# Member matrices of a graph attention layer: from compares on VectorE to bf16 products on TensorE

## Chip, cores and metric

The kernel runs on one core of a Trainium2 chip. The metric is device microseconds of one execution, the lower the better; the median of several runs is compared.

## What is computed

There are 50,000 nodes x 128 features and 50,000 edges, sorted by target node. The reference, cut to what matters:

```python
h = jnp.maximum(_layernorm(x), 0.0)
q = (h @ Wq + bq).reshape(n, H, C); k = ...; v = ...        # H = 4 heads of C = 32
alpha = jnp.einsum('ehc,ehc->eh', q[dst], k[src]) / math.sqrt(C)
ea = jnp.exp(alpha - segment_max(alpha, dst)[dst])
alpha = ea / (segment_sum(ea, dst)[dst] + 1e-16)
x = x + segment_sum(v[src] * alpha[:, :, None], dst) + (h @ Wskip + bskip)
h = jnp.maximum(_layernorm(x), 0.0)
x = x + second_layer(h)    # W, gathered rows, edge features, sums by target node
```

"Layer 1" of the change's name is the attention layer (the first layer below). The second layer isn't touched.

## The kernel before

**Stages.** The *table stage* loads rows of x in 40 batches (`b`), takes layernorm statistics, projects k and v and stores them to DRAM (`kv_rows`); SP's queue carries its loads and stores (L509, L518) in an order written by hand (`for b in range(PB)`), and DVE and POOL make the index tables beside it (`index_work`, `table_stat_math`). The *first layer* then goes through 500 tiles of 100 target nodes; the edges of a tile lie in one window of 128 edges. Ten tiles make a batch, so there are 50 batches. The *second layer* follows.

**The member matrix.** For each tile, `member` [128 edges, 100 nodes] has a 1 where the edge's target is the node. DVE builds it by an is_equal of the edge's relative node (`drel_all`) against an iota: `members`, L1187, for four and for six tiles. PE turns it (`turn_member`, L1891, f32 transposes of groups of 4, 4 and 2 tiles), ACT copies the result from PSUM to `memberT` (`copy_member`, L1666). memberT gathers each edge's q row by a product (`gather_q`, L1903), and member sums the weighted v rows by node (`aggregate`, L1936).

**The order.** Every engine has a function `step0(k)` that lists what it does in step k, and this list is its order: nothing moves past an instruction that waits. One step has work of three batches: k+1 (front: q and members), k (scores) and k-1 (softmax, sums). Each batch's road is: ACT's relu of the normalised rows (L1644), PE's `turn_h` (L1865), ACT's `copy_h` (L1651), PE's `project_q` (bias L1878, product L1882), ACT's `copy_q` (L1658), members and turned members, `gather_q`; DVE's `scores` (L1199) and `head_sums` (L1207) against rows that POOL gathers by indirect DMA (L809, ten per batch); PE's `turn_alpha` (L1910); DVE's eight soft steps (L1222, 1225, 1229, then L1231 to L1241), with ACT's exp (L1672) between the third, numbered 2, and the fourth, numbered 3; PE's `turn_weights` (L1914); DVE's `weigh` (L1247); PE's `skip` (L1923, L1928) and `aggregate` per group; DVE's `finish` (L1259). In every second step DVE also has 14 small steps of layernorm statistics between these.

**Semaphores and banks.** PE raises `A.item` ("front_ready") once for each front product and ACT raises `A.evac` ("front_copied") once for each copy; the numbers within a batch are in `ITEM`. Front products use PSUM banks 0, 1 and 2; a product waits until ACT has copied what stood in the bank:

```python
wait(pe, A.evac, N_ITEM * (k - 1) + ITEM[("m1", "m2")[i]])    # turn_h: banks 0 and 1
wait(pe, A.evac, N_ITEM * (k - 1) + ITEM["q2"])               # project_q, first group: bank 2
```

## Time and profile before

| | |
|---|---|
| median of three runs | 1654.79 us (1652.82, 1654.79, 1658.01) |
| the profiled execution, its span | 1654.16 us, 1652.2 us |
| busy over the span | PE 1468.2 us (89%), DVE 1348.9 (82%), POOL 1082.5 (66%), ACT 1017.2 (62%) |
| granted TensorE clock, mean | 0.979 of full speed |
| first gather of the first layer, and of the second | 301.86 us, 1007.87 us |

Busy shares are means over stages that differ; the rows further below are from single stages. In a timeline a row holds the start, the duration, engine, line, operation, output and input, the count of instructions put together in it, and in brackets the idle time of the engine ahead of it and what ended it. "f32" and "bf16" are the types of the operands; PE's ends are modelled, so neighbouring rows overlap.

### The profile page before, as it was taken

What the parts mean: (1) busy time and instruction counts of PE and PEld (TensorE: products, weight loads), DVE (VectorE), ACT (ScalarE), POOL (GpSimd) and SP (SyncE); (2) the same over time, 40 slices, a digit from 0 to 9 for tenths busy, and PEclk for the clock granted to TensorE, in tenths of its full rate; (3) what the DMA queues carried; (4) which work ended last, traced back from release to release, by engine and by line L of the source; (5) the groups of instructions that cost most, each with busy time, mean ns of one, the idle gap of its engine ahead of it and who ended that gap; (6) DMA issues with size and microseconds to landing.
All of it is one profiled execution on the core that took longest, in us unless ns stands there. A gap on an engine that the chain in (4) does not pass through costs nothing. (4 is left out here: it accounts for less than half of the span.)

```text
span 1652.2 us, 34442 instructions
## 1 busy us (share of the span) xinstructions
PE 1468.2 (89%) x10545; PEld 1262.1 (76%) x10546; DVE 1348.9 (82%) x3688; ACT 1017.2 (62%) x2501; POOL 1082.5 (66%) x1202
## 2 busy tenths in 40 slices
PE   5888888699999999999999984899999999999898
PEld 4667767588888888888888873777777777777776
DVE  8879665299999999999999995677777777777676
ACT  5778888555565655555555622556666666656564
POOL 2554442577777777777777704777777777777774
PEclk9999999899999999999999996999999999999999
DMA  8898888556666666666666616576767666676673
GB/s 217 275 276 309 288 296 268 160 150 184 186 182 186 179 190 174 189 170 187 174 181 181 174 44 164 129 173 163 171 161 162 166 161 159 165 165 159 152 171 94
DMA packets 162552, 302.85 MB, mean 183 GB/s; under 512 B 104113, under 2 KB 107703, under 8 KB 157524
## 3 DMA queue, kind: packets, MB, share of 16 engines
q1 hardware_dynamic: 121503, 201.19, 42.2%
q0 software_dynamic: 40896, 99.90, 24.5%
q8 instruction: 62, 1.02, 0.3%
q14 instruction: 91, 0.75, 0.1%
HBM read 196.84 MB, written 104.12 MB: 182 GB/s over the span
## 5 line engine op out<-in xcount | busy, mean ns | idle before, releaser
L809 POOL DMA_INDIRECT sb_kv<-kv_rows,sb_src_all x500 | 492.9, 986 | 187.4 <-issue 130.7
L837 POOL DMA_INDIRECT sb_kv<-x_rows,sb_src_all x500 | 473.2, 946 | 205.7 <-issue 109.7
L1716 ACT ACTIVATE sb_hn<-sb_xn 100x128 f32<-100x128 f32 x500 | 240.6, 481 | 261.2 <-DMA sb_kv<-x_rows,sb_src_all 198.0
L1719 ACT ACTIVATE sb_vw<-sb_kv 128x128 f32<-128x128 f32 x500 | 239.5, 479 | 0.0
L1644 ACT ACTIVATE sb_hn<-sb_xn,sb_nstat 100x128 f32<-100x128 f32 x500 | 231.5, 495 | 0.0
L1406 DVE COPY sb_hT<-ps_b 128x400 f32<-128x400 f32 x250 | 142.5, 570 | 95.1 <-PE ps_b L2011 93.1
L1803 PE MATMUL ps_b<-sb_w,sb_memberT 128*125 128x256 f32 x800 | 201.2, 390 | 20.0 <-DVE sb_xn L927 12.0
L1666 ACT COPY sb_memberT<-ps_b 100x512 f32<-100x512 f32 x150 | 75.8, 506 | 205.9 <-PE ps_b L1891 205.9
L1803 PEld LDWEIGHTS ps_b<-sb_w,sb_memberT 128*125 128x125 f32 x800 | 146.0, 193 | 43.2 <-issue 16.8
L2011 PE MATMUL ps_b<-sb_member,sb_vw 128*128 128x100 f32 x1000 | 173.5, 278 | 0.0
L2011 PEld LDWEIGHTS ps_b<-sb_member,sb_vw 128*128 128x128 f32 x1000 | 157.0, 198 | 9.8 <-issue 9.8
L2010 PE MATMUL ps_b<-sb_ident,sb_hn 100*128 100x100 f32 x500 | 129.3, 259 | 34.2 <-ACT sb_vw L1719 33.9
L1396 DVE TENSOR_SCALAR sb_member<-sb_iota,sb_drel_all,sb_wdeg_all 128x100 f32<-128x100 f32 x500 | 145.8, 344 | 0.0
L1903 PE MATMUL ps_b<-sb_q,sb_memberT 100*128 100x128 f32 x1000 | 129.4, 276 | 9.5 <-DVE sb_prod L1199 7.6
L1882 PE MATMUL ps_b<-sb_w,sb_hT 128*100 128x128 f32 x1000 | 136.3, 276 | 0.0
L1928 PE MATMUL ps_b<-sb_w,sb_hT 128*100 128x128 f32 x1000 | 136.2, 276 | 0.0
L1882 PEld LDWEIGHTS ps_b<-sb_w,sb_hT 128*100 128x100 f32 x1000 | 126.5, 170 | 5.3
L1928 PEld LDWEIGHTS ps_b<-sb_w,sb_hT 128*100 128x100 f32 x1000 | 126.2, 170 | 5.1
L1903 PEld LDWEIGHTS ps_b<-sb_q,sb_memberT 100*128 100x128 f32 x1000 | 120.1, 192 | 10.4 <-issue 8.2
L1936 PE MATMUL ps_b<-sb_vw,sb_member 128*100 128x128 f32 x1000 | 125.5, 273 | 0.0
L1422 DVE COPY sb_q<-ps_b 128x400 f32<-128x400 f32 x150 | 75.3, 502 | 60.7 <-PE ps_b L2024 60.7
L1602 ACT ACTIVATE sb_q<-sb_kv,sb_pstat 125x128 f32<-125x128 f32 x280 | 119.0, 488 | 7.2 <-DVE sb_pstat L877 7.2
(184 smaller groups left out, 3101.5 us busy)
## 6 DMA issues: line engine op xcount, KB each, us to landing
kv_rows<-sb_kv SPq DMA_DIRECT2D x26, 1120.0 KB
sb_xn<-x_rows SPq DMA_DIRECT2D x50, 507.8 KB
sb_xn<-in_x SPq DMA_DIRECT2D x50, 500.0 KB
out_rows<-sb_xo SPq DMA_DIRECT2D x49, 500.0 KB
x_rows<-sb_xo SPq DMA_DIRECT2D x24, 1015.6 KB
sb_kv<-in_edge_attr SPq DMA_DIRECT2D x500, 32.0 KB
sb_kv<-in_x SPq DMA_DIRECT2D x28, 560.0 KB
kv_rows<-sb_xn SPq DMA_DIRECT2D x13, 1120.0 KB
```

Of the source, the lines that this page charges most:

```text
L809: pool.indirect_dma_start(out=kvs[:, k % 4, t, :], out_offset=None, in_=kv_rows, in_offset=bass.IndirectOffsetOnAxis(ap=src_all[:, n:n + 1 ...
L837: pool.indirect_dma_start(out=xs1[:, k % 4, t, :], out_offset=None, in_=x1, in_offset=bass.IndirectOffsetOnAxis(ap=src_all[:, n:n + 1], ax ...
L1396: ins = dve.tensor_scalar(member[:, (k + 3) % 4, t, :], iota[:], drel_all[:, n:n + 1], wdeg_all[:, n:n + 1], ALU.is_equal, ALU.mult)
L1406: dve.tensor_copy(haT[:, j // 2, :, at:at + 2, :], banks[n % 2][:, 0:4 * NODES].rearrange("c (h t n) -> c h t n", h=2, t=2)).then_inc(R.ha ...
L1644: nc.scalar.activation(hn[:, t, :], xn[:, k % 5, t, :], ACT.Relu, scale=nstat[:, n, 0:1], bias=nstat[:, n, 1:2]).then_inc(A.relu, 1)
L1716: nc.scalar.activation(hn1[:, t, :], xn1[:, k % 4, t, 0:D], ACT.Relu, scale=xn1[:, k % 4, t, D:D + 1], bias=xn1[:, k % 4, t, D + 1:XW]).th ...
L1719: nc.scalar.activation(hs1[:, t, :], xs1[:, k % 4, t, 0:D], ACT.Relu, scale=xs1[:, k % 4, t, D:D + 1], bias=xs1[:, k % 4, t, D + 1:XW]).th ...
L1803: ins = nc.tensor.matmul(banks[2 + n % 4][0:ROWS, (t % 2) * 2 * D:(t % 2 + 1) * 2 * D], hpT[:, (3 * b + g) % 4, (t - first) * ROWS:(t - fi ...
L1882: ins = nc.tensor.matmul(ps[0:NODES, (t - first) * D:(t - first + 1) * D], hnT[:, k % 3, t, :], w0[:, 0, :], start=False, stop=t == last - 1)
L1903: ins = nc.tensor.matmul(banks[3 + a % 2][:, (t - first) * D:(t - first + 1) * D], memberT[:, k % 2, t, :], qsb[:, k % 2, t, :], start=Tru ...
L1928: nc.tensor.matmul(ps[0:NODES, (t - first) * D:(t - first + 1) * D], hnT[:, k % 3, t, :], w0[:, 3, :], start=False, stop=False)
L2011: ins = nc.tensor.matmul(banks[n % 2][:, at + 2 * NODES:at + 3 * NODES], hs1[:, t, :], member[:, (k + 3) % 4, t, :], start=True, stop=True)
```

## The change

The member matrix becomes relu(1 - (e - c)^2), where e is the edge's relative node and c the node, both less 50: 1 where they are equal, 0 elsewhere. Written out, -e^2 + 2ce + (1 - c^2) is a product of an edge factor and a node factor. `edge_part` [128, 13, 128] holds for each batch 32 rows: ten of e^2's bf16 head, ten of its rest, ten of e and two of ones; four batches share the 128 rows of a column. `node_part` [128, 4, 10, 100] has -1, -1 and 2c on the rows of a tile, 1 - c^2 (head and rest) on the last two, and zeros on the rows of the other batches, so that a product runs over all 128 rows.

- PE: `turned_member` makes the turned matrix by a bf16 product per tile where a transpose stood; `row_member`, new, makes the plain matrix by two bf16 products of 500 columns into banks 2 and 0.
- ACT: `copy_member` becomes a Relu; `member_rows`, new, takes the two 500-column products by a Relu into `member`, at the end of ACT's step.
- DVE: `members` and both its calls go.
- Waits: `turn_h` of the first half now waits for the copy M1, `project_q` of the first group for M0, `aggregate` of the first group for its own batch's M1.
- `gather_q(k, 2)` moves ahead of `project_q(k + 1, 0)`.
- Preparation in the table stage: POOL fills (`node_parts`), DVE makes one row and the parts of e (`const_row`, `drel_part`), SP gets 31 transfers: 1, 3, 3 and 24 at b = 23, 25, 27 and 29.

Some buffers move to make room (`brow`, `bpart`, `masked`).

```diff
-N_ITEM = 8
-ITEM = {"h0": 1, "h1": 2, "q0": 3, "q1": 4, "m0": 5, "q2": 6, "m1": 7, "m2": 8}
+N_ITEM = 10
+ITEM = {"h0": 1, "h1": 2, "q0": 3, "q1": 4, "m0": 5, "q2": 6, "m1": 7, "m2": 8, "M0": 9, "M1": 10}
+MID = NODES // 2
+QUADS = 4
+CELL = 32
+COLS = (BATCHES + QUADS - 1) // QUADS
...
+        edge_part = sb("edge_part", [128, COLS, WIN], BF16)
+        node_part = sb("node_part", [128, QUADS, B, NODES], BF16)
...
+            def const_rows_in():
+                sp.wait_ge(node_part_made, 6)
+                sp.wait_ge(const_row_step, 5)
+                sp.dma_start(node_part[3 * B:CELL, 0, :, :].rearrange("j t n -> j (t n)"),
+                             const_rows.rearrange("o j t n -> o j (t n)")).then_inc(const_row_in, 16)
+
+            def node_parts_in():
+                sp.wait_ge(const_row_in, 16)
+                for quad in range(1, QUADS):
+                    sp.dma_start(node_part[CELL * quad:CELL * (quad + 1), quad, :, :], node_part[0:CELL, 0, :, :]
+                                 ).then_inc(node_part_in, 16)
+
+            def drel_parts_out():
+                sp.wait_ge(drel_part_step, 6)
+                for j in range(3):
+                    sp.dma_start(part_rows[j].rearrange("(g r) e -> r g e", r=ROWS),
+                                 drel_parts[:, j, :].rearrange("r (g e) -> r g e", g=TG)).then_inc(drel_part_out, 16)
+
+            def edge_parts_in():
+                sp.wait_ge(drel_part_out, 16 * 3)
+                for quad in range(QUADS):
+                    cols = (BATCHES - quad + QUADS - 1) // QUADS
+                    for j in range(3):
+                        for first, last in ((0, cols - 1), (cols - 1, cols)):
...
+                if b == 23:
+                    const_rows_in()
+                if b == 25:
+                    node_parts_in()
+                if b == 27:
+                    drel_parts_out()
+                if b == 29:
+                    edge_parts_in()
...
             for m in range(EARLY, PAIRS):
                 table_stat_math(m)
+                if m in (8, 9, 10):
+                    for n in ((0, 1), (2, 3), (4, 5))[m - 8]:
+                        node_parts(n)
...
+                if n == 0:
+                    ins = dve.tensor_scalar(mid_drel, drel_f.rearrange("r g e -> r (g e)"), -1.0, NODES + 1.0,
+                                            ALU.max, ALU.min)
...
+                if m == 6 and n < 5:
+                    const_row(n)
...
+                if m == 12 and n < 6:
+                    drel_part(n)
...
-            def members(k, part):
...
-                dve.tensor_tensor(member[:, k % 3, first:last, :],
...
                 stats(4)
-                if nxt:
-                    members(k + 1, 0)
                 stats(5)
...
                 stats(13)
-                if nxt:
-                    members(k + 1, 1)
                 if prev:
                     finish(k - 1, 0)
...
-                nc.scalar.copy(memberT[:, k % 2, first:last, :],
-                               banks[(1, 0, 1)[g]][0:NODES, 0:(last - first) * WIN]
-                               .rearrange("n (t e) -> n t e", e=WIN)).then_inc(A.evac, 1)
+                nc.scalar.activation(memberT[:, k % 2, first:last, :],
+                                     banks[(1, 0, 1)[g]][0:NODES, 0:(last - first) * WIN]
+                                     .rearrange("n (t e) -> n t e", e=WIN), ACT.Relu).then_inc(A.evac, 1)
+
+            def member_rows(k, i):
+                first, last = HALVES[i]
+                act.wait_ge(A.item, N_ITEM * k + ITEM[f"M{i}"])
+                wait(act, A.agg, 3 * (k - 2))
...
+                nc.scalar.activation(member[:, k % 3, first:last, :],
+                                     banks[(2, 0)[i]][:, 0:5 * NODES].rearrange("e (t n) -> e t n", n=NODES),
+                                     ACT.Relu).then_inc(A.evac, 1)
...
                 relus(k + 2, 9, 10)
+                if nxt:
+                    member_rows(k + 1, 0)
+                    member_rows(k + 1, 1)
...
             def turn_h(k, i):
                 first, last = HALVES[i]
                 pe.wait_ge(A.relu, B * k + last)
-                wait(pe, A.evac, N_ITEM * (k - 1) + ITEM[("m1", "m2")[i]])
+                wait(pe, A.evac, N_ITEM * (k - 1) + ITEM[("M1", "m2")[i]])
...
                 if g == 0:
-                    wait(pe, A.evac, N_ITEM * (k - 1) + ITEM["q2"])
+                    wait(pe, A.evac, N_ITEM * (k - 1) + ITEM["M0"])
...
-            def turn_member(k, g):
+            def turned_member(k, g):
                 first, last = FOURS[g]
-                pe.wait_ge(A.member, 2 * k + (1, 2, 2)[g])
+                of_edge, of_node = parts(k)
+                if k == 0 and g == 0:
+                    pe.wait_ge(const_row_in, 16)
+                    pe.wait_ge(node_part_in, 16 * (QUADS - 1))
+                    pe.wait_ge(edge_part_in, 16 * 6 * QUADS)
                 pe.wait_ge(A.evac, N_ITEM * k + ITEM[("h1", "q1", "m0")[g]])
                 for t in range(first, last):
-                    ins = nc.tensor.transpose(banks[(1, 0, 1)[g]][0:NODES, (t - first) * WIN:(t - first + 1) * WIN],
-                                              member[:, k % 3, t, :], ident[:])
+                    ins = nc.tensor.matmul(banks[(1, 0, 1)[g]][0:NODES, (t - first) * WIN:(t - first + 1) * WIN],
+                                           of_node[:, t, :], of_edge, start=True, stop=True)
                 ins.then_inc(A.item, 1)
+
+            def row_member(k, i):
+                first, last = HALVES[i]
+                of_edge, of_node = parts(k)
+                pe.wait_ge(A.evac, N_ITEM * k + ITEM[("q2", "m1")[i]])
+                nc.tensor.matmul(banks[(2, 0)[i]][:, 0:5 * NODES].rearrange("e (t n) -> e t n", n=NODES),
+                                 of_edge, of_node[:, first:last, :], start=True, stop=True).then_inc(A.item, 1)
...
                 pe.wait_ge(A.vw, k + 1)
+                if g == 0:
+                    pe.wait_ge(A.evac, N_ITEM * k + ITEM["M1"])
...
                     turn_h(k + 1, 0)
                     turn_h(k + 1, 1)
-                    project_q(k + 1, 0)
                 if this:
                     gather_q(k, 2)
                 if nxt:
+                    project_q(k + 1, 0)
                     project_q(k + 1, 1)
-                    turn_member(k + 1, 0)
+                    turned_member(k + 1, 0)
                     project_q(k + 1, 2)
...
                 if nxt:
-                    turn_member(k + 1, 1)
-                    turn_member(k + 1, 2)
+                    turned_member(k + 1, 1)
+                    turned_member(k + 1, 2)
+                    row_member(k + 1, 0)
                     gather_q(k + 1, 0)
+                    row_member(k + 1, 1)
                     gather_q(k + 1, 1)
```

PE's order in a step of the first layer before, from the turn of alpha to the second group's projection of q (sb_hn the normalised rows, sb_q the projected q):

```order
L1910 MATMUL ps_b<-sb_ident,sb_alpha 40x128
L1891 MATMUL ps_b<-sb_ident,sb_member 100x128 x6
L1903 MATMUL ps_b<-sb_q,sb_memberT 128x128 x8
L1865 MATMUL ps_b<-sb_ident,sb_hn 128x100 x10
L1878 MATMUL ps_b<-sb_bsplit,sb_ones_b 100x512
L1882 MATMUL ps_b<-sb_w,sb_hT 100x128 x4
L1903 MATMUL ps_b<-sb_q,sb_memberT 128x128 x2
L1878 MATMUL ps_b<-sb_bsplit,sb_ones_b 100x512
L1882 MATMUL ps_b<-sb_w,sb_hT 100x128 x4
```

The same place in the changed kernel, where sb_edge_part and sb_node_part are the two factors:

```order
L2044 MATMUL ps_b<-sb_ident,sb_alpha 40x128
L2018 MATMUL ps_b<-sb_edge_part,sb_node_part 100x128 x6
L2026 MATMUL ps_b<-sb_node_part,sb_edge_part 128x500
L2037 MATMUL ps_b<-sb_q,sb_memberT 128x128 x4
L2026 MATMUL ps_b<-sb_node_part,sb_edge_part 128x500
L2037 MATMUL ps_b<-sb_q,sb_memberT 128x128 x4
L1985 MATMUL ps_b<-sb_ident,sb_hn 128x100 x10
L2037 MATMUL ps_b<-sb_q,sb_memberT 128x128 x2
L1998 MATMUL ps_b<-sb_bsplit,sb_ones_b 100x512
L2002 MATMUL ps_b<-sb_w,sb_hT 100x128 x4
L1998 MATMUL ps_b<-sb_bsplit,sb_ones_b 100x512
L2002 MATMUL ps_b<-sb_w,sb_hT 100x128 x4
```

Between the member turns and the gathers stand two products of 500 columns now, and the third group's gather (the row of two) stands ahead of the projection's bias.

ACT's order before, from the last relus of one step to the exp of the next (sb_memberT the turned member matrix, sb_hT the turned rows, sb_er the exps):

```order
L1644 ACTIVATE sb_hn<-sb_xn,sb_nstat 100x128 x3
L1666 COPY sb_memberT<-ps_b 100x512
L1644 ACTIVATE sb_hn<-sb_xn,sb_nstat 100x128
L1666 COPY sb_memberT<-ps_b 100x256
L1644 ACTIVATE sb_hn<-sb_xn,sb_nstat 100x128
L1651 COPY sb_hT<-ps_b 128x500 x2
L1644 ACTIVATE sb_hn<-sb_xn,sb_nstat 100x128
L1672 ACTIVATE sb_er<-sb_dl 40x128
```

and in the changed kernel:

```order
L1748 ACTIVATE sb_hn<-sb_xn,sb_nstat 100x128 x3
L1770 ACTIVATE sb_memberT<-ps_b 100x512
L1748 ACTIVATE sb_hn<-sb_xn,sb_nstat 100x128
L1770 ACTIVATE sb_memberT<-ps_b 100x256
L1748 ACTIVATE sb_hn<-sb_xn,sb_nstat 100x128
L1783 ACTIVATE sb_member<-ps_b 128x500 x2
L1755 COPY sb_hT<-ps_b 128x500 x2
L1748 ACTIVATE sb_hn<-sb_xn,sb_nstat 100x128
L1789 ACTIVATE sb_er<-sb_dl 40x128
```

The two 128x500 rows into sb_member are new between a step's last relu and the next step's copies of the turned rows.

DVE's order before, around the place where it needs the exps (sb_dl their input):

```order
L1225 SCALAR_TENSOR_TENSOR sb_smax<-sb_segk,sb_fmax 40x128
L1229 TENSOR_TENSOR sb_dl<-ps_b,sb_smax 40x128
L1187 TENSOR_TENSOR sb_member<-sb_drel_all,sb_iota 128x400
L1231 SCALAR_TENSOR_TENSOR sb_fsum<-sb_segk,sb_er 40x128
L1233 SCALAR_TENSOR_TENSOR sb_tot<-sb_segk,sb_fsum 40x128
```

and in the changed kernel:

```order
L1333 SCALAR_TENSOR_TENSOR sb_smax<-sb_segk,sb_fmax 40x128
L1337 TENSOR_TENSOR sb_dl<-ps_b,sb_smax 40x128
L1339 SCALAR_TENSOR_TENSOR sb_fsum<-sb_segk,sb_er 40x128
L1341 SCALAR_TENSOR_TENSOR sb_tot<-sb_segk,sb_fsum 40x128
L1344 TENSOR_SCALAR sb_tot_e<-sb_tot 40x128
```

The compare that stood between the last step ahead of the exp and the first one behind it is gone.

## Rows read from the trace of the kernel before

**Rows 1.** Busy time by window, first layer: window, length, engines busy (instructions), PEclk, DMA share, GB/s.
```profile
500.00:600.00 100.00, 94.09 (x806) 87.89 (x805) 97.42 (x269) 58.06 (x139) 76.25 (x78) 1.00 0.65 183
```
**Rows 2.** Timeline of POOL, 902 to 932 us: start, duration, then as said above.
```profile
902.60 1.58 POOL L809 DMA_INDIRECT sb_kv<-kv_rows,sb_src_all  x1 [0.30 <-issue]
...
921.48 0.95 POOL L809 DMA_INDIRECT sb_kv<-kv_rows,sb_src_all  x1 [0.30 <-issue]
...
929.40 1.58 POOL L809 DMA_INDIRECT sb_kv<-kv_rows,sb_src_all  x1 [0.30 <-issue]
```
**Rows 3.** Groups by line and shape, 400 to 900 us: busy us, mean ns, idle before, releasers.
```profile
L809 POOL DMA_INDIRECT sb_kv<-kv_rows,sb_src_all x384 | 379.1, 987 | 123.0 <-issue 100.2 <-PE ps_b L1903 8.7 <-PE ps_b L1891 6.1
L1644 ACT ACTIVATE sb_hn<-sb_xn,sb_nstat 100x128 f32<-100x128 f32 x375 | 174.1, 495 | 0.0
...
L1259 DVE TENSOR_TENSOR sb_xo<-ps_b,sb_xn 100x512 f32<-100x512 f32 x74 | 47.3, 679 | 0.0
...
L1666 ACT COPY sb_memberT<-ps_b 100x512 f32<-100x512 f32 x75 | 43.4, 579 | 156.9 <-PE ps_b L1891 156.9
...
L1187 DVE TENSOR_TENSOR sb_member<-sb_drel_all,sb_iota 128x600 f32<-128x600 f32 x37 | 28.6, 772 | 0.0
L1187 DVE TENSOR_TENSOR sb_member<-sb_drel_all,sb_iota 128x400 f32<-128x400 f32 x37 | 20.6, 558 | 0.0
...
L1666 ACT COPY sb_memberT<-ps_b 100x256 f32<-100x256 f32 x37 | 13.3, 360 | 0.0
```
**Rows 4.** Timeline of PE, 603.5 to 615 us.
```profile
604.13 0.25 PE L1914 MATMUL ps_b<-sb_ident,sb_wr 40*128 40x40 f32 x1 [0.41 <-DVE sb_wr L1241]
604.32 0.42 PE L1923 MATMUL ps_b<-sb_bsplit,sb_ones_b 128*100 128x512 bf16 x1
604.57 1.04 PE L1928 MATMUL ps_b<-sb_w,sb_hT 128*100 128x128 f32 x8
...
606.53 1.91 PE L1936 MATMUL ps_b<-sb_vw,sb_member 128*100 128x128 f32 x16
608.93 0.31 PE L1923 MATMUL ps_b<-sb_bsplit,sb_ones_b 128*100 128x256 bf16 x1 [0.48 <-DVE sb_xo L1259]
...
610.06 0.82 PE L1891 MATMUL ps_b<-sb_ident,sb_member 128*100 128x128 f32 x6
...
612.50 1.02 PE L1865 MATMUL ps_b<-sb_ident,sb_hn 100*128 100x100 f32 x10
```
**Rows 5.** Timeline of ACT, 610 to 616 us.
```profile
610.69 0.58 ACT L1666 COPY sb_memberT<-ps_b 100x512 f32<-100x512 f32 x1 [4.64 <-PE ps_b L1891]
611.17 0.49 ACT L1644 ACTIVATE sb_hn<-sb_xn,sb_nstat 100x128 f32<-100x128 f32 x1
611.57 0.36 ACT L1666 COPY sb_memberT<-ps_b 100x256 f32<-100x256 f32 x1
611.82 0.50 ACT L1644 ACTIVATE sb_hn<-sb_xn,sb_nstat 100x128 f32<-100x128 f32 x1
613.13 1.05 ACT L1651 COPY sb_hT<-ps_b 128x500 f32<-128x500 f32 x2 [0.81 <-PE ps_b L1865]
...
614.51 0.31 ACT L1672 ACTIVATE sb_er<-sb_dl 40x128 f32<-40x128 f32 x1
```
**Rows 6.** Timeline of DVE, 600 to 618 us.
```profile
601.53 0.41 DVE L1231 TENSOR_TENSOR_SCAN sb_fsum<-sb_segk,sb_er 40x128 f32<-40x128 f32 x1
...
614.88 0.41 DVE L1231 TENSOR_TENSOR_SCAN sb_fsum<-sb_segk,sb_er 40x128 f32<-40x128 f32 x1
...
617.01 0.28 DVE L1241 TENSOR_TENSOR sb_wr<-sb_er,sb_rtot 40x128 f32<-40x128 f32 x1
```
**Rows 7.** Busy time by window, end of the table stage, columns as in rows 1.
```profile
200.00:300.00 100.00, 84.82 (x439) 68.70 (x437) 57.98 (x161) 82.21 (x202) 32.32 (x55) 0.98 0.84 282
```
**Rows 8.** Timeline of SP's queue, 225 to 250 us: start, time of the issues.
```profile
230.43 2.38 SPq L509 DMA_DIRECT2D sb_kv<-in_x  x2
238.78 0.75 SPq L518 DMA_DIRECT2D kv_rows<-sb_kv  x2
```

More of the change, by code:

```diff
@@ L397, in __init__ @@
                 self.evac = s("front_copied")
-                self.member = s("member_built")
                 self.qe = s("q_gathered")
@@ L587, in segments_out @@
                              seg_t.rearrange("r g k e -> r g (k e)")).then_inc(seg_out, 16)
+            def const_rows_in():
[19 more added lines that the diff above has]
+                        for first, last in ((0, cols - 1), (cols - 1, cols)):
+                            rows = part_rows[j, B * QUADS * first + B * quad:B * QUADS * (last - 1) + B * (quad + 1), :]
+                            at = CELL * quad + B * j
+                            if last - first == 1:
+                                sp.dma_start(edge_part[at:at + B, first, :], rows).then_inc(edge_part_in, 16)
+                            else:
+                                full = part_rows[j, 0:B * QUADS * last, :]
+                                sp.dma_start(edge_part[at:at + B, first:last, :],
+                                             full.rearrange("(c q t) e -> q t c e", q=QUADS, t=B)[quad]
+                                             ).then_inc(edge_part_in, 16)
             def nodes(k):
@@ L976, in split_biases @@
             def split_biases(n):
-                flat = brow[:].rearrange("o j n -> o (j n)")[:, 0:5 * D]
+                flat = brow.rearrange("o j n -> o (j n)")[:, 0:5 * D]
                 if n == 0:
@@ L1132, in window_cols, with const_row, drel_part @@
                 ins.then_inc(idx_all, 1)
+            def const_row(n):
+                wait(dve, const_row_step, n)
+                if n == 0:
+                    ins = dve.tensor_scalar(mid_node, iota[0:1, :], -float(MID), None, ALU.add)
+                elif n == 1:
+                    ins = dve.tensor_tensor(mid_square, mid_node, mid_node, ALU.mult)
+                elif n == 2:
+                    ins = dve.tensor_scalar(mid_node, mid_square, -1.0, 1.0, ALU.mult, ALU.add)
+                elif n == 3:
+                    ins = dve.tensor_copy(const_rows[:, 0, :, :], mid_node.unsqueeze(1).to_broadcast([1, B, NODES]))
+                else:
+                    ins = dve.tensor_tensor(const_rows[:, 1, :, :], mid_node.unsqueeze(1).to_broadcast([1, B, NODES]),
+                                            const_rows[:, 0, :, :], ALU.subtract)
+                ins.then_inc(const_row_step, 1)
+            def drel_part(n):
+                wait(dve, drel_part_step, n)
+                if n == 0:
+                    ins = dve.tensor_scalar(mid_drel, drel_f.rearrange("r g e -> r (g e)"), -1.0, NODES + 1.0,
+                                            ALU.max, ALU.min)
+                elif n == 1:
+                    ins = dve.tensor_scalar(mid_drel, mid_drel, -float(MID), None, ALU.add)
+                elif n == 2:
+                    ins = dve.tensor_copy(drel_parts[:, 2, :], mid_drel)
+                elif n == 3:
+                    ins = dve.tensor_tensor(drel_square, mid_drel, mid_drel, ALU.mult)
+                elif n == 4:
+                    ins = dve.tensor_copy(drel_parts[:, 0, :], drel_square)
+                else:
+                    ins = dve.tensor_tensor(drel_parts[:, 1, :], drel_square, drel_parts[:, 0, :], ALU.subtract)
+                ins.then_inc(drel_part_step, 1)
             def index_work(m, n):
@@ L1179, in _ @@
                 table_pair(m)
-            def members(k, part):
-                first, last = ((0, 4), (4, B))[part]
-                dve.wait_ge(idx_all, 3)
-                if k == 1:
-                    dve.wait_ge(seg_out, 16)
-                wait(dve, A.agg, 3 * (k - 2))
-                dve.tensor_tensor(member[:, k % 3, first:last, :],
-                                  drel_all[:, B * k + first:B * k + last].unsqueeze(2)
-                                  .to_broadcast([128, last - first, NODES]),
-                                  iota[:].unsqueeze(1).to_broadcast([128, last - first, NODES]), ALU.is_equal
-                                  ).then_inc(A.member, 1)
             def scores(k, g):
                 first, last = FOURS[g]
+                if k == 0 and g == 0:
+                    dve.wait_ge(idx_all, 3)
                 if g == 0:
@@ L1286, in step0 @@
             def step0(k):
-                this, prev, nxt = real(k), real(k - 1), real(k + 1)
+                this, prev = real(k), real(k - 1)
                 m = (k - 3) // 2
```

43 lines of the change are left out of this document (40 added, 3 removed).

## The prediction

> **What bounds the kernel now.** I read the busy time by window first, then the timelines of single engines in one batch, then the groups by line. The kernel has a table stage (to about 300 us), the first layer (to about 1000 us) and the second layer; only the first two change. In the first layer DVE is busy 97.42 us of 100 and PE 94.09, while ACT has 58.06 and POOL 76.25 [rows 1]: the reader is to see that DVE has 2.58 us of idle time in 100 and so sets the pace. The pace is read from POOL's gathers: two of them that stand at the same place of their batches, two batches apart, start 26.80 us apart [rows 2], so a batch takes 13.40 us. POOL by itself would be quicker: a gather of 0.95 with 0.30 ahead of it [rows 2] is 1.25 us, and ten are 12.5 us a batch. DVE spends 0.558 + 0.772 = 1.33 us per batch on the member matrix [rows 3], of 0.9742 x 13.40 = 13.05 us busy.
>
> **What the change does to each engine, per batch of the first layer.**
> - DVE loses the two compares: 13.05 - 1.33 = 11.72 us busy. If DVE alone set the pace, a batch would drop by about 1.3 us.
> - PE loses ten f32 turns and gets ten bf16 products and two of 500 columns. From 16 products in 1.91 us and six turns in 0.82 [rows 4] ten f32 matmuls cost 1.09 us, 0.109 each. A bf16 matmul of 512 columns lets the next one start after 604.57 - 604.32 = 0.25 us [rows 4]. A bf16 one of 128 columns stands nowhere in the trace; its bounds are a quarter of 0.25 (0.06) and 0.109. I take the middle, 0.086. So PE gets 0.86 + 0.50 - 1.09 = +0.27: from 0.9409 x 13.40 = 12.61 to 12.88 us. It still fits in 13.40.
> - ACT gets two ACTIVATEs of 128x500 and six dearer links. 58% of 13.40 is 7.8 us, so as an engine it has room. But its instructions stand in one order, and the two new ones stand behind the last relu of a step and ahead of the next step's copies of h. PE's turns of h now wait for the second of them (M1), since it reads the bank they write.
> - POOL keeps its ten gathers, 12.5 us by its own pace.
>
> **The loop that takes over.** Follow what releases what, once round, with the present rows:
> (a) from the turn of the weights (L1914) over skips and products to the last group's skip: PE goes 604.13 to 606.53 (2.40), its first eight products take 7 x 0.109 + 0.27 = 1.04, DVE's finish 0.68 [rows 3, 4], two hand-overs of 0.04: 4.20. PE's own issue to the end of all 16 products gives the same.
> (b) skip, products and turn of alpha to the member turns: 608.93 to 610.06, 1.13 [rows 4].
> (c) member turns to ACT's first copy: 610.69 - 610.06 = 0.63 now [rows 4, 5], of which four turns are 3 x 0.109 + 0.27. In bf16 the tail of one is 0.42 - 0.19 = 0.23 (the 512-column row less three quarters of its spacing [rows 4]), so 0.26 + 0.23 + 0.03 = 0.52; ends 0.44 and 0.63.
> (d) ACT in its order: copy, relu, copy 610.69 to 611.82 = 1.13, relu 611.57 - 611.17 = 0.40, and the two new ones. At the price of the two 500-column COPYs they take 1.05 [rows 5]. Sum 2.58.
> (e) PE's turns of h, ACT's two copies and a relu to the exp: 612.50 to 614.51, 2.01 [rows 4, 5], and a hand-over: 2.05.
> (f) exp 0.31 and hand-over: 0.35 [rows 5].
> (g) DVE's soft steps 3 to 7 until the next turn of the weights: 614.88 to 617.01 + 0.28 + 0.04 = 2.45; with statistics between them 601.53 to 604.13 = 2.60 [rows 4, 6]. They alternate: 2.53.
> Together 13.36 us. Today the two new links are not in the ring, so it is 13.36 - 1.05 + 0.11 (the slower turns) = 12.4 us, a microsecond short of DVE's pace, and does not show.
>
> **The unknown price in the ring** is what an ACTIVATE Relu from PSUM costs over a COPY; four of them lie in (d). COPY rises from 360 to 579 ns over 256 columns [rows 3], 0.86 ns a column, which makes 250 at 128. Nothing, or even a gain, is the one end (nothing excludes a gain, but both read and write the same tiles). For the other the exp, an ACTIVATE without row operands, takes 310 [rows 5]: 0.06 more. I take 0.02, since COPY has the tile's shape and the PSUM source. So the ring is 13.36 + 0.08 = 13.44 us against 13.40. Over some 47 batches (50 less the filling) that is **+2 us**. DVE's relief is eaten: 1.3 us leave its line, and a ring of 13.4 stands behind it. What DVE gains becomes idle time ahead of soft step 3.
>
> The third q group is gathered ahead of the next batch's projection. DVE could have waited for it at most in its 2.58 idle us of 100, 0.35 a batch [rows 1]; but the turns of h, now later, still stand ahead of it, and the ring does not pass it: 0, ends -0.35 and 0 a batch, and only if DVE were the bound.
>
> The Trainium skill ("ScalarE: Activation LUTs", "Rules for kernel authors") says that relu belongs on VectorE and budgets some 0.3 us per ACTIVATE (bias as a pointer operand) plus 0.83 ns per element. By it the four links would be an estimated 0.57 us dearer than the COPY rows, and the time about 1682. The trace speaks against that size: the exp of 128 columns has 310 ns, not 410.
>
> **Table stage.** DVE gets 11 small steps and POOL six fills, both in a stretch where DVE was busy 57.98 of 100 us and POOL 32.32 [rows 7]: 0, since both wait for the loads there. If the cover failed, the DVE steps would cost some 6 us at the price of a finish (0.68) each. SP's queue gets 31 more transfers. Two issues took 0.75 us [rows 8], so 31 are 11.6 us. After a pair of loads ends at 232.81 the queue is idle until 238.78, 5.97 us [rows 8], and that recurs with every pair; but 24 of the 31 stand in one place (b = 29) and push the loads behind them. The data (0.38 MB out, 0.38 in) take 2.7 us at the 282 GB/s of this stretch [rows 7]. I take **+2.5 us**; ends 0 and 12.
>
> **Sum:** the profiled execution took 1654.16 us (span 1652.2), 0.6 below the median of the runs, 1654.79. 1654.16 + 2 + 2.5 = **1658.6 us**. About 0.3%, 5 us, is what a measurement here can tell from nothing. The own range of this case: with 0.44 in (c), 2.45 for (g) and a Relu that is 0.02 cheaper than COPY the ring is 13.12, -13 us, and with a table stage at 0 the time is 1641; with 0.63, 2.60 and 0.06 it is 13.78, +18, and 2.5 make 1675.
>
> **Rivals.**
> - *POOL becomes the bound (faster).* If (a) and (g) hold delays that the compares cause, the ring shrinks with them. Both gathers that are long (1.58 against 0.95 [rows 2]) stand at the same place of a batch; and the mean of 987 ns [rows 3] against 0.95 says that lengthening costs POOL some 14 us over 384 gathers. The Trainium skill ("GPSIMD Engine Reference", "1. Specifications") says GpSimd contends with VectorE instructions that have two SBUF inputs, which the compares have; the 1.58 agrees. The batch would fall to 12.5 or 12.6: 0.85 x 47 = 40 us, about **1617**. It needs the ring below 12.6, 0.8 under my sum, and my terms are mostly engines' own work in order.
> - *ACT's links are dear (slower).* If Relu from PSUM is priced like the other Relus in this layer, 495 ns at 128 columns [rows 3] against COPY's 250, each link costs 0.245 more, the ring is 14.34: +44 + 2.5, **1700**; with 0.06 it starts at 1675. It decides the sign from 0.023 a link, where the sum passes +5 us. Against it: those rows take scale and bias from columns in SBUF, the new ones don't.
> - *SP's queue is exposed (slower).* All 31 issues on the path: +12 (at the 1.19 each of the loads [rows 8] 24 would be 28.6, less two gaps 17): with +2, about **1670**.
> - *The change does not do what it says.* That third group is sooner only in order. Worth 0, so it stays inside the forecast.
>
> **How the numbers follow.** Forecast 0.70 (own range 1641 to 1675), POOL bound 0.10, dear links 0.12, SP exposed 0.08. The forecast's range splits: 0.14 below -5 us, 0.34 within, 0.22 above. Faster 0.10 + 0.14 = 0.24; same 0.34; slower 0.22 + 0.12 + 0.08 = 0.42. The range from 1641 to 1688 (middle of the dear links' 1675 to 1700) leaves out POOL's case and half of the dear links, 0.16, and the forecast's tails.
>
> **What would show it.** Right: in the first layer gathers at the same place of their batches, two apart, 26.9 us apart; all gathers near 0.95; DVE busy some 87 of 100 and idle for ACT's exp ahead of soft step 3; PE idle for ACT's second member row ahead of the turns of h; Relu of 512 columns at 0.58 to 0.64. Wrong: gathers back to back at 1.25 (POOL's case), Relu of 500 columns at 0.7 or more (dear links), the table stage over 5 us longer (SP's), or PE idle nowhere while its turns of h start as before, which would mean that the ring is not what holds the batch.

## The result, and the profile after

The changed kernel took 1664.14 us (median of 12 runs, 1661.31 to 1666.01) against 1656.97 for the kernel before (12 runs, 1651.54 to 1662.81): a ratio of 1.0041, 95% interval 1.0028 to 1.0055. It is slower by some 7 us. The profiled execution took 1662.34 us with a span of 1660.6, 8.4 more than before.

Two rows of POOL's timeline say where, the first gather of the first layer and that of the second; the weight loads of PE's turns of the weights, one in each of 50 batches, give the first and the last (ns least, median and most, then the starts; first the changed kernel, then the kernel before):

```profile
316.31 1.10 POOL L891 DMA_INDIRECT sb_kv<-kv_rows,sb_src_all  x1 [28.70 <-DMA kv_rows<-sb_kv]
...
1017.44 0.94 POOL L919 DMA_INDIRECT sb_kv<-x_rows,sb_src_all  x1 [52.42 <-DMA x_rows<-sb_xo]
```
```profile
L2048 PEld LDWEIGHTS ps_b<-sb_ident,sb_wr x50: 133/135/138, 348.2 to 997.8; 40*128 40x128 f32 x50
```
```profile
L1914 PEld LDWEIGHTS ps_b<-sb_ident,sb_wr x50: 134/135/180, 334.5 to 987.4; 40*128 40x128 f32 x50
```

The table stage ends 316.31 - 301.86 = 14.45 us later. From the first gather to the second layer's the first layer takes 701.1 us where it took 706.0: 4.9 less, of which 3.3 lie between the first and the last turn of the weights (649.6 for 652.9). What follows takes 643.2 for 644.3; nothing was changed there. 14.45 - 4.9 - 1.1 = 8.4.

In the first layer DVE is no longer full (busy time by window, columns as in [rows 1]; then groups by line, 400 to 900 us, as in [rows 3]):

```profile
500.00:600.00 100.00, 93.78 (x827) 87.86 (x826) 91.09 (x268) 65.80 (x158) 75.87 (x80) 1.00 0.65 186
```
```profile
L891 POOL DMA_INDIRECT sb_kv<-kv_rows,sb_src_all x386 | 366.1, 949 | 136.1 <-issue 82.6 <-DVE sb_vw L1355 17.8 <-PE ps_b L2018 10.0
...
L1770 ACT ACTIVATE sb_memberT<-ps_b 100x512 f32<-100x512 f32 x75 | 44.3, 591 | 129.3 <-PE ps_b L2018 125.9 <-issue 3.4
L1783 ACT ACTIVATE sb_member<-ps_b 128x500 f32<-128x500 f32 x74 | 39.1, 586 | 0.0
L1755 ACT COPY sb_hT<-ps_b 128x500 f32<-128x500 f32 x74 | 39.0, 579 | 29.7 <-PE ps_b L1985 29.7
L1985 PE MATMUL ps_b<-sb_ident,sb_hn 100*128 100x100 f32 x370 | 38.8, 252 | 16.4 <-ACT sb_member L1783 16.4
...
L1339 DVE TENSOR_TENSOR_SCAN sb_fsum<-sb_segk,sb_er 40x128 f32<-40x128 f32 x37 | 15.5, 418 | 24.1 <-ACT sb_er L1789 24.1
```

Before, the last two of these had no idle time ahead of them:

```profile
L1865 PE MATMUL ps_b<-sb_ident,sb_hn 100*128 100x100 f32 x370 | 37.8, 249 | 0.0
...
L1231 DVE TENSOR_TENSOR_SCAN sb_fsum<-sb_segk,sb_er 40x128 f32<-40x128 f32 x37 | 15.1, 409 | 0.0
```

DVE has 91.09 of 100 where it had 97.42. Its idle time stands where the forecast put it: 24.1 us over 37 batches, 0.65 each, ahead of soft step 3, ended by ACT's exp; and PE waits 16.4 / 37 = 0.44 us per batch ahead of the turns of h for ACT's member row. All gathers are short (949 ns).

One round of the ring, first PE, then ACT, then DVE (timelines, as in [rows 4 to 6]):

```profile
601.66 0.25 PE L2048 MATMUL ps_b<-sb_ident,sb_wr 40*128 40x40 f32 x1 [0.32 <-DVE sb_wr L1349]
...
605.88 0.31 PE L2057 MATMUL ps_b<-sb_bsplit,sb_ones_b 128*100 128x256 bf16 x1
...
607.01 0.50 PE L2018 MATMUL ps_b<-sb_edge_part,sb_node_part 128*100 128x128 bf16 x6
607.35 0.37 PE L2026 MATMUL ps_b<-sb_node_part,sb_edge_part 128*128 128x500 bf16 x1
...
610.16 1.05 PE L1985 MATMUL ps_b<-sb_ident,sb_hn 100*128 100x100 f32 x10 [0.44 <-ACT sb_member L1783]
...
615.09 0.25 PE L2048 MATMUL ps_b<-sb_ident,sb_wr 40*128 40x40 f32 x1 [0.45 <-DVE sb_wr L1349]
```
```profile
607.44 0.60 ACT L1770 ACTIVATE sb_memberT<-ps_b 100x512 f32<-100x512 f32 x1 [3.41 <-PE ps_b L2018]
...
608.97 1.06 ACT L1783 ACTIVATE sb_member<-ps_b 128x500 f32<-128x500 f32 x2
...
612.16 0.30 ACT L1789 ACTIVATE sb_er<-sb_dl 40x128 f32<-40x128 f32 x1
```
```profile
612.49 0.42 DVE L1339 TENSOR_TENSOR_SCAN sb_fsum<-sb_segk,sb_er 40x128 f32<-40x128 f32 x1 [0.34 <-ACT sb_er L1789]
```

| link | forecast | here |
|---|---|---|
| (a) weights to last skip | 4.20 | 605.88 - 601.66 = 4.22 |
| (b) to member turns | 1.13 | 607.01 - 605.88 = 1.13 |
| (c) to ACT's first Relu | 0.52 | 607.44 - 607.01 = 0.43 |
| (d) ACT's six | 2.58 + 0.08 | 608.97 + 1.06 - 607.44 = 2.59 |
| (e) turns of h to exp | 2.05 | 612.16 - 610.03 = 2.13 |
| (f) exp to soft step 3 | 0.35 | 0.33 |
| (g) soft steps to weights | 2.53 (2.60 with statistics) | 615.09 - 612.49 = 2.60 |
| batch | 13.44 | 13.43 |

The links are laid end to end, so their sum is this batch's length by construction; what shows that they hold one another are the waits in brackets.

### The profile page after: what moved, and what is told of

Same layout as the page of the kernel before. It is cut to its first block and busy times, and to the rows that moved or that the text cites. A ratio compares the mean times of both kernels' runs of the same rounds, so it can differ in the third digit from the quotient of the medians.

```text
span 1660.6 us, 34596 instructions
## 1 busy us (share of the span) xinstructions
PE 1462.6 (88%) x10645; PEld 1257.9 (76%) x10646; DVE 1308.4 (79%) x3599; ACT 1055.6 (64%) x2601; POOL 1074.9 (65%) x1208
## 5 line engine op out<-in xcount | busy, mean ns | idle before, releaser
L891 POOL DMA_INDIRECT sb_kv<-kv_rows,sb_src_all x500 | 474.1, 948 | 203.3 <-issue 108.6
L1923 PE MATMUL ps_b<-sb_w,sb_memberT 128*125 128x256 f32 x800 | 205.5, 396 | 28.0 <-DVE sb_xn L1009 14.8
L1770 ACT ACTIVATE sb_memberT<-ps_b 100x512 f32<-100x512 f32 x150 | 77.6, 518 | 169.4 <-PE ps_b L2018 166.0
L2037 PE MATMUL ps_b<-sb_q,sb_memberT 100*128 100x128 f32 x1000 | 137.9, 277 | 6.1 <-DVE sb_prod L1307 6.0
L2037 PEld LDWEIGHTS ps_b<-sb_q,sb_memberT 100*128 100x128 f32 x1000 | 131.9, 193 | 9.1 <-issue 6.4
```

What stands on the lines that cost most here:

```text
L891: pool.indirect_dma_start(out=kvs[:, k % 4, t, :], out_offset=None, in_=kv_rows, in_offset=bass.IndirectOffsetOnAxis(ap=src_all[:, n:n + 1 ...
L1923: ins = nc.tensor.matmul(banks[2 + n % 4][0:ROWS, (t % 2) * 2 * D:(t % 2 + 1) * 2 * D], hpT[:, (3 * b + g) % 4, (t - first) * ROWS:(t - fi ...
L2037: ins = nc.tensor.matmul(banks[3 + a % 2][:, (t - first) * D:(t - first + 1) * D], memberT[:, k % 2, t, :], qsb[:, k % 2, t, :], start=Tru ...
```

## Experiments

Each kernel left a profile; a ratio is to runs of the kernel before on the same chip. A batch's length is taken between turns of the weights 20 and 46 (26 batches), the first gather from POOL's timeline. The kernels ran on several chips, so differences between two of them are taken from the ratios (0.001 is 1.7 us).

| kernel | first gather, us | a batch, us | median, us | ratio to before (95%) |
|---|---|---|---|---|
| before | 301.86 | 13.41 | 1656.97 | 1 |
| changed | 316.31 | 13.41 | 1664.14 | 1.0041 (1.0028 to 1.0055) |
| e1 relus early | 316.00 | 12.90 | 1646.28 | 0.9956 (0.9943 to 0.9969) |
| e2 members static | 304.10 | 12.95 | 1631.94 | 0.9853 (0.9826 to 0.9879) |
| e3 preparation only | 315.73 | 13.41 | 1667.09 | 1.0074 (1.0050 to 1.0098) |
| e4 parts late | 315.05 | 13.41 | 1663.09 | 1.0053 (1.0035 to 1.0071) |
| e5 parts by POOL | 309.38 | 13.42 | 1655.96 | 0.9994 (0.9980 to 1.0008) |
| e6 relus early, parts by POOL | 310.19 | 12.90 | 1640.14 | 0.9893 (0.9875 to 0.9911) |
| e7 banks exchanged | 313.03 | 13.04 | 1652.81 | 0.9968 (0.9957 to 0.9978) |
| e8 q group put back | 314.68 | 13.42 | 1664.13 | 1.0042 (1.0027 to 1.0058) |
| e9 no edge parts | 305.70 | 13.42 | 1654.45 | 0.9992 (0.9976 to 1.0008) |
| e10 no preparation | 300.56 | 13.42 | 1651.02 | 0.9974 (0.9959 to 0.9989) |
| e11 all three | 311.68 | 13.01 | 1646.59 | 0.9933 (0.9908 to 0.9958) |

**Is it the ring? e1, e7, e2, e11.**

e1 moves two relus out of the ring into time in which ACT waits:

```diff
-                relus(k + 2, 5, 8)
+                relus(k + 2, 5, 10)
                 if nxt:
                     copy_member(k + 1, 1)
-                relus(k + 2, 8, 9)
-                if nxt:
                     copy_member(k + 1, 2)
-                relus(k + 2, 9, 10)
```

> The changed kernel with the last two relus of ACT's step moved ahead of the copy of the second group of turned members, where ACT now waits 3.4 us for PE; the same work, another order. Ring theory (the first layer is paced by the ring in which ACT's two member rows hold PE's turns of h): the two relus take 0.38 + 0.39 = 0.77 us out of the ring, a batch falls from 13.38 us to about 12.65, some 35 us in all, near 1629. Rival, PE's own work and waits set the pace whatever ACT does: PE stays at 13.4 and the time at 1664. Rival, the ring gives way but POOL's gathers end it: 12.5 to 12.55 us a batch, near 1624.

The time fell with the same work done, by 14 us by the ratios (1.0041 to 0.9956), so ACT's order paced the first layer, as the ring has it. The size was missed: a batch fell to 12.90, not 12.65. Its batches alternate between 12.73 and 13.04. PE now goes from the gather behind the second product into the turns of h with no wait, as these rows of e1's PE timeline show:

```profile
799.98 0.38 PE L2023 MATMUL ps_b<-sb_node_part,sb_edge_part 128*128 128x500 bf16 x1
800.20 1.05 PE L2034 MATMUL ps_b<-sb_q,sb_memberT 100*128 100x128 f32 x8
801.12 1.05 PE L1982 MATMUL ps_b<-sb_ident,sb_hn 100*128 100x100 f32 x10
```

In the window from 600 to 900 us PE is busy 288.32 us of 300 and DVE 282.29; POOL, with 223.32, isn't the limit:

```profile
600.00:900.00 300.00, 288.32 (x2560) 272.73 (x2559) 282.29 (x805) 207.40 (x490) 223.32 (x237) 1.00 0.66 186
```

One batch near the start takes 18.78 us in e1: 5 to 6 us lost once. In e6, which has the same order and one of 18.42, DVE's timeline shows what it waits for there, gathered rows:

```profile
380.35 1.29 DVE L1307 TENSOR_TENSOR sb_prod<-ps_b,sb_kv 128x512 f32<-128x512 f32 x2 [4.92 <-DMA sb_kv<-kv_rows,sb_src_all]
```

e7 leaves ACT's order and changes which of the two copies the turns of h wait for; the first group's gather moves ahead of both products with it:

```diff
-                wait(pe, A.evac, N_ITEM * (k - 1) + ITEM[("M1", "m2")[i]])
+                wait(pe, A.evac, N_ITEM * (k - 1) + ITEM[("M0", "m2")[i]])
...
-                nc.tensor.matmul(banks[(2, 0)[i]][:, 0:5 * NODES].rearrange("e (t n) -> e t n", n=NODES),
+                nc.tensor.matmul(banks[(0, 2)[i]][:, 0:5 * NODES].rearrange("e (t n) -> e t n", n=NODES),
...
-                    row_member(k + 1, 0)
                     gather_q(k + 1, 0)
+                    row_member(k + 1, 0)
                     row_member(k + 1, 1)
```

> The changed kernel with the banks of the two new products exchanged and the one of bank 0 made and copied first (PE makes both after the first group's gather): the turns of h wait for the first of ACT's two member rows, not the second; ACT's order and work stay. Ring theory: the turns of h start one copy (0.48 us) sooner, a batch takes about 12.95 us, 20 us less, near 1644; no less, since with the relus moved the next limit was 12.9. Rival, the relus of the first run gained by something else than the wait of the turns of h (sooner rows of h for the next batch): no change, 1664.

13.04 us a batch and 12 us less by the ratios: the wait of the turns of h is part of the pace, by another edit than e1's. The gain is less than the 20 us expected. It too has one batch of 18.79 us near the start, and its batches alternate between 12.83 and, for the most part, 13.28, where 13.05 would give 12.94, near the 12.95 expected; the last section shows what goes with the 13.28.

e2 prices the relief of DVE without anything in its place:

```diff
-                if nxt:
+                if nxt and k < 2:
                     members(k + 1, 0)
...
-                pe.wait_ge(A.member, 2 * k + (1, 2, 2)[g])
+                pe.wait_ge(A.member, 2 * min(k, 2) + (1, 2, 2)[g])
```

> The kernel before, with the compares only for the first three batches; later batches use these stale member matrices, so the sums are not the reference's. Nothing takes the compares' place on PE or ACT. It prices DVE's relief without the new ring. Ring theory: without the two new links the ring is 12.4 us, so the next limit is POOL (12.5) or PE, 12.5 to 12.65 us a batch against 13.43: 37 to 44 us faster than before, near 1616. Rival, DVE was not what paced the first layer: within 5 us of before, 1657.

24 us faster: the compares did pace the first layer, and the change could have earned that. It is less than the 37 to 44 expected: again the next limit is 12.95, where I had read POOL's 12.5. None of its gathers is longer than 1.2 us; before there were 34, and in e3, which has the compares, 33 (ns least, median and most, first before, then e2):

```profile
L809 POOL DMA_INDIRECT sb_kv<-kv_rows,sb_src_all x500: 940/946/1591, 301.9 to 953.3; - x167
```
```profile
L809 POOL DMA_INDIRECT sb_kv<-kv_rows,sb_src_all x500: 940/946/1110, 304.1 to 934.2; - x167
```

So the compares lengthen the gathers; that this costs time is not shown, as POOL isn't the limit with them or without.

e11 puts e1, e5 and e7 together.

> The last two relus moved ahead, the transfers on POOL's queue, and the banks of the two new products exchanged. In the run with the relus alone PE went without a wait from the second product into the turns of h, so ACT's member rows no longer held it and the ring ran over PE's own work, 12.73 us, and in the steps with statistics over DVE, 13.04. So the sooner release buys nothing: 12.85 to 12.95 us a batch, 1638 to 1643. If ACT's member rows still hold it: 12.4 to 12.6 a batch, near 1622.

Nothing is gained over e6: 13.01 us a batch against 12.90, and 1646.59 us, over the 1638 to 1643 expected. PE has no wait for ACT's member rows ahead of the turns of h, so with the relus early they no longer hold the ring. The tenth of a microsecond over e6 lies in batches of 13.28 as in e7.

**Where do 14 us of the table stage come from? e3, e10, e4, e5, e9.**

> The changed kernel's preparation (POOL's fills, DVE's row and parts, SP's 31 transfers, the moved buffers) with the first layer of the kernel before: compares on DVE, turns, copies, order as before; the prepared factors are not used. If the preparation is the whole loss: the first gather at about 316 us against 302, and the time 12 to 15 us over before, near 1670. If it is the first layer that loses and the later first gather is caught up there: within 5 us of before, near 1657.

```diff
-                if nxt:
-                    member_rows(k + 1, 0)
-                    member_rows(k + 1, 1)
...
+                if nxt:
+                    members(k + 1, 0)
```

(and so back, line by line, in the rest of the first layer.) The first gather at 315.73 and 12 us over before: the preparation is the whole loss, and more than the changed kernel's 7. e10 is the counterpart:

```diff
-                    for n in ((0, 1), (2, 3), (4, 5))[m - 8]:
-                        node_parts(n)
+                    if m == 8:
+                        pool.memset(node_part[:], 0.0).then_inc(node_part_made, 1)
+                    if m == 9:
+                        pool.memset(edge_part[:], 1.0).then_inc(node_part_made, 1)
...
-                if m == 12 and n < 6:
-                    drel_part(n)
```

> The changed kernel's first layer with nothing of the preparation but two fills: no transfers, no DVE steps; the factors hold zeros and ones, so the member matrices are not the reference's. The table stage is then that of the kernel before: first gather at 301 to 304 us, and the time shows the first layer's change alone: 4 to 6 us faster than before by the traces (from the first turn of the weights to the last 649.6 us against 652.9, and some earlier start), near 1651. If the first layer of the change is slower by itself, as the sum of the forecast has it (+2): 1657 to 1660.

The first gather is back at 300.56 and the time is 1651.02, 0.26% under before: the first layer's change alone gains 4 to 5 us. +12 and -4 give +8, near the measured +7.

SP's timeline in the changed kernel shows the transfers in its queue, and the windows what the DMA engines did meanwhile:

```profile
194.29 1.28 SPq L612 DMA_DIRECT2D sb_node_part<-sb_xo  x1
...
205.93 4.25 SPq L618 DMA_DIRECT2D sb_node_part<-sb_node_part  x3
...
218.74 10.86 SPq L624 DMA_DIRECT2D part_rows<-sb_xo  x3
229.64 1.83 SPq L529 DMA_DIRECT2D sb_hT<-in_x  x2
...
238.41 0.34 SPq L639 DMA_DIRECT2D sb_edge_part<-part_rows  x1
...
249.82 0.34 SPq L636 DMA_DIRECT2D sb_edge_part<-part_rows  x1
250.21 0.76 SPq L529 DMA_DIRECT2D sb_kv<-in_x  x2
```
```profile
220.00:230.00 10.00, 8.10 (x44) 6.62 (x43) 6.28 (x22) 7.60 (x20) 1.64 (x8) 1.00 0.68 229
...
260.00:270.00 10.00, 2.79 (x9) 2.12 (x7) 3.77 (x14) 1.99 (x6) 0.98 (x5) 0.65 0.89 263
```

and in the kernel before:

```profile
220.00:230.00 10.00, 8.70 (x46) 6.83 (x46) 5.65 (x19) 8.73 (x22) 3.54 (x9) 1.00 0.96 350
260.00:270.00 10.00, 9.64 (x53) 8.08 (x52) 8.59 (x28) 9.51 (x24) 3.45 (x10) 1.00 0.97 307
```

The node factor's four issues hold the queue for 5.5 us, the three of the parts of e for 10.86, and the 24 reads take 11.8 from the first to the last: 28 us for all 31. The loads behind them start late: the DMA share falls to 0.68 from 220 us on, where it was 0.96, and PE, which projects the loaded rows, is busy 2.79 of 10 us from 260 us on, where it was 9.64. e4 moves them to where no load follows:

```diff
-                if b == 27:
+                if b == 34:
                     drel_parts_out()
-                if b == 29:
+                if b == 36:
                     edge_parts_in()
```

> The changed kernel with the 27 transfers of the edge parts moved on SP's queue from b = 27 and 29 to b = 34 and 36, where no table load is left behind them. Theory of the queue (the loads behind the transfers start late and starve the table stage): the first gather comes at 303 to 307 us in place of 316, and the time falls by 9 to 13 us, near 1653. Rival, load on the DMA engines (3000 runs of 256 B take their time wherever they stand): the first gather stays at 313 to 318 us, the time at 1661 to 1666.

The number is that of the rival (315.05), but its reading doesn't follow. SP's timeline shows the last stores of kv rows behind the transfers, and POOL's that the first gather waits for these stores:

```profile
271.69 7.90 SPq L624 DMA_DIRECT2D part_rows<-sb_xo  x3
...
297.95 0.34 SPq L636 DMA_DIRECT2D sb_edge_part<-part_rows  x1
298.39 0.74 SPq L538 DMA_DIRECT2D kv_rows<-sb_kv  x2
```
```profile
315.05 1.10 POOL L891 DMA_INDIRECT sb_kv<-kv_rows,sb_src_all  x1 [36.49 <-DMA kv_rows<-sb_kv]
```
```profile
290.00:300.00 10.00, 8.92 (x47) 7.11 (x45) 4.85 (x7) 6.14 (x16) 0.00 (x0) 1.00 0.29 78
```

From 290 to 300 us the DMA engines were busy only 0.29 of the time, so in that stretch it was the queue and not their load. e4 tested a place in the queue, and both places had something urgent behind. e5 takes all 31 out of the queue:

```diff
-                if b == 27:
-                    drel_parts_out()
...
+                if m == 15:
+                    drel_parts_out()
...
+            edge_parts_in()
+
             def gathers(k):
```

(the same functions with POOL as the issuing engine, ahead of its gathers.)

> The changed kernel with all 31 transfers of the preparation issued from POOL's queue instead of SP's: the same data and the same runs of 256 B, the 24 reads of the edge parts in the 28 us in which POOL waits ahead of its first gather. If the cost is SP's queue, wherever the transfers stand in it (in the run with the parts late the last stores of kv rows waited behind them): the first gather at 301 to 305 us in place of 316, the time near 1652. If it is load on the DMA engines, or POOL's and DVE's part of the preparation: the first gather stays at 311 or later, the time over 1659.

POOL's timeline: the 24 reads take 14.2 us of time in which POOL would wait for the stores anyway, and 12.73 are left.

```profile
282.49 0.70 POOL L857 DMA_DIRECT2D sb_edge_part<-part_rows  x1
...
296.09 0.55 POOL L854 DMA_DIRECT2D sb_edge_part<-part_rows  x1
309.38 1.08 POOL L891 DMA_INDIRECT sb_kv<-kv_rows,sb_src_all  x1 [12.73 <-DMA kv_rows<-sb_kv]
```

About half of the loss of the trace is gone (309.38), and the time is that of before, neither the 1652 of the one case nor over the 1659 of the other. For the rest e9 leaves out the edge parts' transfers as well (against e5's kernel):

```diff
-                if m == 15:
-                    drel_parts_out()
...
-            edge_parts_in()
-
```

> The run with POOL's queue (first gather 309.4 us, 7.5 us after the kernel before) without the 27 transfers of the edge parts out and in; the edge factor stays at its filling of ones, so the member matrices are not the reference's. If the 3000 runs of 256 B are what still costs: the first gather at 302 to 305 us, the time 4 to 7 us below that run's 1656, near 1650. If it is the fills, the node factor's transfers or DVE's steps: it stays at 307 to 311, the time at 1654 to 1657.

305.70, and 1654.45 us. Set in a row: 300.56 (nothing), 305.70 (fills, DVE's steps, the node factor's four transfers), 309.38 (and the 27 transfers, by POOL), 316.31 (all by SP's queue). These are single executions: with one and the same table stage the first gather stood at 316.31, 316.00, 315.73, 314.68 and 313.03, with another at 309.38, 310.19 and 311.68 (e5, e6, e11), and without any preparation at 301.86 and 304.10 (before, e2). So each step is good to 3 us or so, and the means of the first five and the last two, 315.2 and 303.0, make the loss 12 us, as e3's time has it, not 14. The ratios rest on several executions each: 1.0041 (changed), 0.9994 (e5), 0.9992 (e9), 0.9974 (e10). By them SP's queue has 8 of 11 us, the 27 transfers from POOL's queue cost nothing that can be told, and 3 us, near the width of the intervals, are left for the fills, DVE's steps and the node factor's transfers; how these divide stays open.

**The third group's gather, e8.**

```diff
+                if nxt:
+                    project_q(k + 1, 0)
                 if this:
                     gather_q(k, 2)
                 if nxt:
-                    project_q(k + 1, 0)
                     project_q(k + 1, 1)
```

> The changed kernel with the third group's gather of q put back behind the next batch's first projection. The forecast priced this part of the change at nothing: 1661 to 1667. Rival, the sooner gather is a gain that hides in the sum (DVE's third scores come late without it and the turn of the weights with them): 0.2 to 0.35 us a batch, 1673 to 1681.

1664.13: this part of the change is worth nothing, as forecast.

**A version that beats both, e6.**

> The last two relus moved ahead, as in the first run, and the 31 transfers on POOL's queue. If the two costs are separate they add up: 18 us from the relus and 11 to 14 from the queue, 1632 to 1636, a ratio to before of about 0.987. If the table stage's end is caught up in the first layer, or POOL's issues push its gathers: 1643 to 1647 as with the relus alone.

1640.14, a ratio of 0.9893. The time lies between the two expectations. By the ratios it is 10 us under e1, and 24 under the changed kernel, where the relus alone bring 14 (e1) and the queue alone 8 (e5): the two costs add up.

## Why the prediction was right, and where it was not

The sign and the range were right (1664 in 1641 to 1688); the two terms were not, and that the total came so near is luck. The forecast was +4.5 us, +7 was measured: the first layer came out 6 us below its term and the table stage some 10 above, and the two misses cancel in part.

- **The ring** holds the batch, as forecast, and the round shown takes 13.43 us against 13.44. The 0.01 is closer than the terms: (c) and (d) are 0.09 and 0.07 short, (e) and (g) 0.08 and 0.07 long. (c) is short because six bf16 products let the next row start after 0.34 us (607.01 to 607.35), 0.057 each, the lower bound, where the middle, 0.086, was taken. e1 and e7 show by two different edits that the ring paces the first layer, and e2 that DVE's relief alone would have been worth 24 us. That ACT's new links eat it is shown by these and by PE's wait of 0.44 us a batch for ACT's member row.
- **DVE's relief** was sized too high: 87 busy of 100 was the sign, 91.09 came. In 100 us DVE lost 6.33, 0.85 a batch, not 1.33. In part this is because neighbouring DVE rows overlap, so that the sum of two rows takes off too much: this compare ends at 614.96, and the next row starts at 614.88 [rows 6].

```profile
614.40 0.56 DVE L1187 TENSOR_TENSOR sb_member<-sb_drel_all,sb_iota 128x400 f32<-128x400 f32 x1
```

- **The unknown price in the ring**, Relu over COPY, was 591 - 579 and 372 - 360 ns for the copies of turned members and 586 - 579 for the new ones: 0.01 each where 0.02 was taken. By the Trainium skill ("ScalarE: Activation LUTs", "Rules for kernel authors") the links would have been an estimated 0.57 us dearer a batch. The rows speak against it for these Relus, which have no pointer operand, while that budget has the bias as one; a section of the same page, "What ACT_TABLE_LOAD costs", gives 186 ns + 0.833 ns an element for one with immediate scale and bias, an estimated 612 ns at 512 columns, and 591 is near that.
- **The first layer's +2 us** failed in its base, and as much in the ring. I set 13.44 against 13.40, which was read at 902 to 929 us. Batches 2 to 20 of the kernel before take 13.49 on average (they alternate, 13.36 and 13.58), 0.09 over the base; those of the changed kernel take 13.35, 0.09 under the ring. So the first layer became shorter, -4.9 us in the trace, and e10 shows the same alone, -4 to -5. Later, between turns 20 and 46, both take 13.41.
- **The table stage's +2.5 us** was mis-sized: 14.45 by the trace, 12 by e3, at or over the upper end of 12. I had counted 31 issues at 0.37 us, 11.6 in all, and let SP's idle gaps take most. They took 28: the 24 short ones 11.8 by themselves, three issues of 500 runs each 10.86 together, the node factor's four 5.5; and what stands behind them in the queue (loads, and in e4 stores) moved back. The price of an issue was read from the quietest pair of rows; the long issues of loads (2.38 for two [rows 8]) were the better sign. The rival with SP's queue exposed, held at 0.08, is the nearest to what happened.
- **POOL as the bound** is refuted: with the compares gone (e2) or the ring shortened (e1) the batch stops at 12.9 to 12.95, where PE and DVE are busy, not at 12.5.
- **The third q group** at 0: shown by e8.

## What to carry to other kernels

Relieving the busiest engine is worth only the distance to the next ring of waits, so close that ring on paper before moving work to an engine with 40% idle time: an idle engine with a fixed order can still be late at one place, and reordering what already stands there can be worth more than the move. Price one-off preparation by what stands behind it in the issuing queue, and look for a queue that waits anyway. Read a period from several stretches of a stage before subtracting a forecast from it.

## What the runs showed of the hardware that was not expected

A small DVE instruction takes longer at a fixed distance behind the start of one of POOL's gathers. The add of 1e-16 to the sums (soft step 5, 40x128 f32, L1344; L1236 before) takes 0.22 us or, as a rule, 0.32 to 0.47, and which of them goes with when it starts: between 400 and 900 us of the changed kernel the 25 long cases start 0.55 to 0.83 us after a gather's start, and the 13 short cases at 0.24 to 0.49 or 0.93 to 1.11. In the kernel before the 10 long cases start at 0.58 to 0.63, the 28 short cases at 0.48 to 0.49 or from 1.23 on. In e2 four cases of 0.28 to 0.29 us start at 1.21 to 1.22, so the band is not the only place. No run moved the gathers alone: that they are the cause is inferred from the distance. The spread over all batches (ns least, median, most), first in the changed kernel, then before, then in e7, and one long case with its gather, from DVE's and POOL's rows:

```profile
L1344 DVE TENSOR_SCALAR sb_tot_e<-sb_tot x50: 218/335/442, 346.7 to 996.2; 40x128 f32<-40x128 f32 x50
```
```profile
L1236 DVE TENSOR_SCALAR sb_tot_e<-sb_tot x50: 218/219/408, 333.0 to 985.9; 40x128 f32<-40x128 f32 x50
```
```profile
L1344 DVE TENSOR_SCALAR sb_tot_e<-sb_tot x50: 218/218/465, 343.4 to 982.3; 40x128 f32<-40x128 f32 x50
```
```profile
868.16 0.34 DVE L1344 TENSOR_SCALAR sb_tot_e<-sb_tot 40x128 f32<-40x128 f32 x1
```
```profile
867.51 0.95 POOL L891 DMA_INDIRECT sb_kv<-kv_rows,sb_src_all  x1 [0.30 <-issue]
```

It stands in link (g) of the ring, and the batch follows it. Batches 4 to 45, with statistics or without, take in the changed kernel 13.29 to 13.34 us where the add is short, 13.41 to 13.43 where it takes 0.32 to 0.35 (nearly all from the 20th on) and 13.51 to 13.52 where it takes 0.43 to 0.44. It goes with two other steps of this text. The batches with statistics of the kernel before take 13.56 to 13.59 with a long add (ten, all in the first half) and 13.44 with a short one (ten, and one of 13.99): the base of 13.40 was read where the add is short. And in e7 and e11 the batches of 13.27 to 13.31 are those with an add of 0.46 or 0.47 (13 and 12 batches); with a short one the same steps take 13.03 to 13.13, as in e1 and e6.
